# Loads of y and x1 and the stores of the output moved to one queue, normalisation one step earlier

## The reference

```
x1  = x  + layernorm(window_attention(layernorm(x) @ w_qkv))
y   = layernorm(x1), looked at as 8192 tokens
g   = mean over a batch's tokens of (relu(y @ gate_w1.T + b) @ gate_w2.T + b)      # 8 numbers a batch
mW1 = W1 + sum_e g[e] * TW1[e];   mW2 = W2 + sum_e g[e] * TW2[e]                    # per batch
out = x1 + layernorm(gelu(y @ mW1.T + mb1) @ mW2.T + mb2)
```

## Time and profile before

| | |
|---|---|
| median of 3 runs | 3098.09 us |
| profiled execution, its time | 3096.61 us |
| its span, first to last instruction | 3094.8 us |
| mean granted TensorE clock | 0.973 of full speed |
| TensorE busy, share of the span | 94% |
| VectorE, ScalarE, GpSimd busy | 64%, 49%, 28% |
| SyncE's DMA queue, ScalarE's, GpSimd's: MB moved | 631, 138, 34 |

### The profile page before, as it was taken

How to read it: one execution, slowest core, us unless ns; L and a number is a source line. 1 busy time by engine, 2 the same in 40 slices (tenths; PEclk the granted TensorE clock), 3 DMA queues, 4 the chain that set the end, 5 groups by cost and what they waited for, 6 DMA issues and landing times. The chain is left out here.

```text
span 3094.8 us, 55878 instructions
## 1 busy us (share of the span) xinstructions
PE 2912.5 (94%) x20402; PEld 2416.9 (78%) x20402; DVE 1986.4 (64%) x3730; ACT 1503.6 (49%) x2918; POOL 865.4 (28%) x725
## 2 busy tenths in 40 slices
PE   7999999789999999949986999989999999999997
PEld 5888888578888888837764888878888888888886
DVE  4333333278878888858747777788668766887412
ACT  2222222166666667645532554554445544554444
POOL 0000000178888888843310000140004100230004
PEclk9999999889999999979997999999999999999999
DMA  5554554568877777769979999999989988999533
GB/s 190 176 176 163 179 195 166 163 166 195 195 182 195 191 190 199 174 192 364 370 274 352 387 389 348 361 367 403 348 301 354 368 306 314 362 376 362 196 105 123
DMA packets 436839, 805.98 MB, mean 260 GB/s; under 512 B 28520, under 2 KB 160616, under 8 KB 436600
## 3 DMA queue, kind: packets, MB, share of 16 engines
q1 hardware_dynamic: 358208, 630.94, 61.6%
q10 hardware_dynamic: 69696, 138.42, 12.5%
q0 software_dynamic: 8704, 33.56, 3.0%
HBM read 634.51 MB, written 167.78 MB: 259 GB/s over the span
## 5 line engine op out<-in xcount | busy, mean ns | idle before, releaser
L1461 DVE SCALAR_TENSOR_TENSOR e_part<-ring,e_g_cols,e_part 128x512 f32<-128x512 f32 x896 | 649.3, 783 | 16.8 <-DMA ring<-mix_rows 13.8
L666 DVE TENSOR_REDUCE b_neg_max<-b_ps_score 128x1 f32<-128x384 f32 (+1 forms) x1024 | 491.8, 527 | 69.0 <-PE b_ps_score L531 57.4
L1372 ACT ACTIVATE e_u<-e_hid,e_mb 128x512 f32<-128x512 f32 x256 | 176.6, 690 | 636.0 <-PE e_hid L1314 631.4
L637 ACT ACTIVATE b_probs<-b_ps_keys 128x384 f32<-128x384 f32 (+1 forms) x1024 | 427.0, 479 | 80.0 <-PE b_ps_keys L546 52.0
L1312 PE MATMUL e_hid<-e_y_hi,e_w_hi 128*128 128x512 f32 x1024 | 402.5, 393 | 33.1 <-DVE e_w_lo L1472 29.9
L1482 DVE TENSOR_TENSOR e_u_lo<-e_u,e_u_hi 128x512 fp32r<-128x512 f32 x256 | 180.6, 706 | 368.2 <-ACT e_u_hi L1376 368.2
L1330 PE MATMUL e_acc<-e_w_hi,e_u_hi 128*128 128x512 f32 x1024 | 400.0, 391 | 11.8 <-ACT e_acc L1396 9.7
L1313 PE MATMUL e_hid<-e_y_lo,e_w_hi 128*128 128x512 f32 x1024 | 401.3, 392 | 0.0
L1314 PE MATMUL e_hid<-e_y_hi,e_w_lo 128*128 128x512 f32 x1024 | 401.2, 392 | 0.0
L1332 PE MATMUL e_acc<-e_w_hi,e_u_lo 128*128 128x512 f32 x1024 | 399.8, 390 | 0.0
L1331 PE MATMUL e_acc<-e_w_lo,e_u_hi 128*128 128x512 f32 x1024 | 399.6, 390 | 0.0
(11 more groups left out here) (123 smaller groups left out, 5112.9 us busy)
## 6 DMA issues: line engine op xcount, KB each, us to landing
ring<-mix_rows SPq DMA_DIRECT2D x576, 512.0 KB, 8.7
e_y_hi<-yh_scratch ACTq DMA_DIRECT2D x66, 1024.0 KB, 10.3
e_y_lo<-yl_scratch ACTq DMA_DIRECT2D x66, 1024.0 KB, 17.1
qk_scratch<-a_qk SPq DMA_DIRECT2D x128, 512.0 KB, 2.7
b_k_st<-qk_scratch SPq DMA_DIRECT2D x192, 256.0 KB, 4.3
b_q_st<-qk_scratch SPq DMA_DIRECT2D x192, 256.0 KB, 4.2
a_x_in<-x SPq DMA_DIRECT2D x16, 1024.0 KB, 7.2
v_scratch<-a_v SPq DMA_DIRECT2D x64, 256.0 KB, 3.0
```

The lines of the kernel that those rows point to most:

```text
L637: act.activation(probs[:, m % RING, h, 0:(hi - lo) * WIN], ps_keys[x % BANKS][:, 0:(hi - lo) * WIN], ACT.Exp, scale=SCALE).then_inc(exp_do ...
L666: dve.tensor_reduce(neg_max[:, g % 2, i, h:h + 1], ps_score[y % BANKS][:, 0:(hi - lo) * WIN], AX_X, ALU.max, negate=True).then_inc(reduced, 1)
L1461: dve.scalar_tensor_tensor(out=part[:, n % 2, half, :], in0=ring[:, i % RING, half * D:(half + 1) * D], scalar=g_cols[:, b, e:e + 1], in1= ...
```

## The change

- All loads of y are issued by SyncE. `load_y(r + 2)` stands behind the refills of step `last[r] - 1`, with a wait for `hidden(last[r])`. ScalarE issues no DMA any more.
- The loads of x1 and the stores of the output are issued by SyncE too: x1 behind the refills of step `last[r]`, with a wait until the adds of the closing run before are done; the stores as four of 256 KB, behind step `last[r] + 5`, each with a wait for its tile's add. Of the last two runs, the stores stand at the end of SyncE's program.
- `normalise` stands at step `last[r] + 2` instead of `+ 3`.

```diff
-        def load_y(eng, r):
-            for src, dst in ((yh_dram, y_hi), (yl_dram, y_lo)):
-                eng.dma_start(dst[:, r % 2].bitcast(F32),
-                              src[:, tokens(r)].rearrange("(k p) t -> p k t", p=P)).then_inc(y_loaded[r % 2], 16)
...
+                def load_y(r):
+                    if r >= 2:
+                        sp.wait_ge(hid_done, last[r - 2] + 1)
+                    for src, dst in ((yh_dram, y_hi), (yl_dram, y_lo)):
+                        sp.dma_start(dst[:, r % 2].bitcast(F32),
+                                     src[:, tokens(r)].rearrange("(k p) t -> p k t", p=P)).then_inc(y_loaded[r % 2], 16)
...
+                def load_x1(r):
+                    if closed_before(r):
+                        sp.wait_ge(added, TILES * closed_before(r))
+                    else:
+                        sp.wait_ge(mb2_stored, 16)
+                    sp.dma_start(x1[:, :, :], x1_dram[tokens(r), :].rearrange("(t p) d -> p t d", p=P)).then_inc(x1_loaded, 16)
+                def store_out(r):
+                    for t in range(TILES):
+                        at = chunk_of(r) * CH + t * P
+                        sp.wait_ge(added, TILES * closed_before(r) + t + 1)
+                        sp.dma_start(out[at:at + P, :], sums[:, runs[r][1], t, :]).then_inc(out_stored, 16)
...
                 for s, (r, jj) in enumerate(steps):
                     refill(upto[s - 1] if s else EXPERTS * START, upto[s])
                     for run in range(RUNS):
+                        if s == last[run] - 1 and run + 2 < RUNS:
+                            load_y(run + 2)
+                        if s == last[run] and closes(run):
+                            load_x1(run)
+                        if s == last[run] + 5 and closes(run):
+                            store_out(run)
...
-                sp.wait_ge(out_stored, 16 * PER * BATCH)
+                for run in range(RUNS):
+                    if last[run] + 5 >= STEPS and closes(run):
+                        store_out(run)
+                sp.wait_ge(out_stored, 16 * TILES * PER * BATCH)
...
-                def load_x1(r):
-                    pool.dma_start(x1[:, :, :], x1_dram[tokens(r), :].rearrange("(t p) d -> p t d", p=P)).then_inc(x1_loaded, 16)
...
-                        pool.wait_ge(added, TILES * (at + 1))
-                        pool.dma_start(out[tokens(r), :].rearrange("(t p) d -> p t d", p=P), sums[:, runs[r][1]]).then_inc(out_stored, 16)
-                        if at + 1 < len(closing):
-                            load_x1(closing[at + 1])
...
-                    r = steps[s][0]
-                    if s == last[r] and r + 2 < RUNS:
-                        load_y(act, r + 2)
...
-                        if s == last[r] + 3 and closes(r):
+                        if s == last[r] + 2 and closes(r):
                             normalise(r)
```

More of the change, by code:

```diff
@@ L1224, in _ @@
                     sp.dma_start(dst, src).then_inc(bias_loaded, 16)
-                load_y(sp, 0)
+                load_y(0)
                 sp.wait_ge(bias_done, BATCH + 1)
@@ L1230, in _ @@
                 refill(0, EXPERTS)
-                load_y(sp, 1)
+                load_y(1)
                 refill(EXPERTS, EXPERTS * START)
@@ L1247, in _ @@
                 pool.wait_ge(const_done, 3)
-                def load_x1(r):
-                    pool.dma_start(x1[:, :, :], x1_dram[tokens(r), :].rearrange("(t p) d -> p t d", p=P)).then_inc(x1_loaded, 16)
-                closing = [r for r in range(RUNS) if closes(r)]
-                pool.wait_ge(mb2_stored, 16)
-                load_x1(closing[0])
                 for r in range(RUNS):
@@ L1383, in copy_out @@
                     if opens(r) and batch_of(r) and t == 0:
-                        act.wait_ge(out_stored, 16 * (PER * (batch_of(r) - 1) + runs[r][1] + 1))
+                        act.wait_ge(out_stored, 16 * TILES * (PER * (batch_of(r) - 1) + runs[r][1] + 1))
                     act.activation(sums[:, runs[r][1], t, :], acc[t][:, :], ACT.Copy).then_inc(copied, 1)
```

## The result

The changed kernel takes 3232.64 us (median of 4 runs, 3218.83 to 3240.12) against 3097.35 us of the kernel before on the same chip. The ratio is 1.0433, with a 95% interval of 1.0394 to 1.0471. The forecast was 3133 us with a range to 3178: the sign was right and the size off by almost four times (35 us expected, 135 measured).

The account below looks back on a forecast made before the run. TensorE was taken as the bound, with the DMA engines right behind in the first batch. Losses 38 + 8 + 10 less gains 21 gave 35 us on 3096.6, so 3131.6, as median 3133; range 3100 to 3178.

Parts of the forecast that it names:

- U: In the last phase, the start of the activation behind the first `hidden` of run r + 1; issue times count from it.
- the 9.7 us wait: TensorE's single wait on an accumulator's start values in the last phase; expected to go, with 2.3 us of half clock.
- The end of the kernel: Last run's adds and store: x1 arriving sooner and a smaller last store would end the span 6.1 us earlier.
- The gains together: Last phase: start-values wait 9.7, its clock 2.3, old waits on y 3.1 and the end 6.1, together 21 us.
- The clock: TensorE's granted clock falling behind ten of the 15 short-run stalls, 1.0 us each: 10 us lost, bounds 0 and 17.
- Short runs: 15 loads of y for 3-step runs: 1.5 us stall each, plus third mix pairs and `low_weights`; 38 us lost.
- Long runs: 51 loads of y for 4-step runs: mostly in time, 8 us lost over 24 with three mix pairs, bounds 0 to 36.
- rival 1: Last phase: stalls on y stay at the lower bound, queue empty, clock holds; no change, 3097 us; chance 0.14.
- rival 2: Last phase: y is on time and the gains stay, so faster, 3077 us; chance 0.07.
- Rival 3: Last phase: y stands behind a queue of ring loads on SyncE's queue, much slower, 3184 us; chance 0.14.
- Rival 4: Last phase: the queue makes no difference, y still lands in 17 to 19 us; over 3350 us; chance 0.03.
- Rival 5: End of the first batch: moving x1 fixes nothing, 12 us more, 3145 us; chance counted within the forecast's 0.62.

Follow-up runs that it names:

- experiment 7: The changed kernel with y issued after the step's last mix but ahead of its two to four ring loads: 3132.49 us, ratio 1.0137.
- experiment 9: The changed kernel with y on SyncE's queue ahead of the refills of step `last[r] - 2`, issued when its buffer comes free: 3075.47 us, ratio 0.9945.
- experiment 10: The same as experiment 9, but with `normalise` back at step `last[r] + 3`: 3073.79 us, ratio 0.9944.
- experiment 5: The kernel before with only `normalise` moved, to step `last[r] + 2`: 3086.51 us, ratio 0.9981.
- experiment 1: The changed kernel with the loads of y back on ScalarE's queue at step `last[r]`, the rest as changed: 3080.84 us, ratio 0.9946.
- experiment 3: The changed kernel with y one step earlier on SyncE's queue, behind the refills of step `last[r] - 2`: 3092.11 us, ratio 0.9986.
- experiment 8: The changed kernel with 180 extra matmuls, 12 ahead of each wait for y in the 15 short-run cases, results thrown away: 3203.19 us, ratio 1.0352.
- experiment 2: The kernel before with only the loads of y moved to SyncE's queue, behind the refills of step `last[r] - 1`: 3238.50 us, ratio 1.0458.

## Why the prediction was wrong in its size

**Right.** When y is needed (U + 13.4), and in 13 of the 15 short-run cases when it is issued (U + 5.1 to 7.6, where the sum had U + 5.4 to 7.9). That all 15 short-run cases stall. That the 9.7 us wait goes. That a load waits for what is ahead on its queue: experiment 7. The end of the kernel came 6.1 us sooner, as forecast, but two errors cancel in it: the last adds start 2.5 us behind `normalise` instead of 1.5, and the span ends 2.5 us behind the adds instead of 3.5. The gains together were put at 21 us; experiments 9 and 10, without the loss, gain 16 to 18 in the median and 21 to 22 in the span of one execution (3073.9 and 3072.5 from 3094.8). Their parts are less sure: the wait and its clock were put at 12 us and gave 5.9 when removed alone (experiment 5).

**The step that failed** is the sum of the losses: 38 + 8 + 10 = 56 us were expected, and the runs showed about 158. The mechanism, a load of y issued too late for TensorE, was right, and experiments 1, 3 and 9 show it; three terms were too small.

*The clock: 10 expected, about 52 measured* (1464.2 us busy within the phase in the changed kernel against 1412.0 in experiment 9, where nothing stalls on y; 2.0 us for each of 26 waits, 2.3 for each of the 23 behind which the clock fell). I had a row that gave 1.7 us for one gap and wrote 1.0 for ten stalls, because a gap of 1.8 us had cost nothing. With the short stalls 2.0 us longer than I thought (67.9 / 15 = 4.5 against 38 / 15 = 2.5) and eleven long ones, the ten became 23. It was the largest error of all, and experiment 8 shows half of it (26.6 us) by itself. My upper bound of 17 us was too low for the same reason. The Trainium skill, page "TensorE: Matmul & The Clock Gate", section "HAM oscillation — how this bites in real kernels", tells of the same loss: a stream of matmuls that waits for data in each round falls back to the slow clock and pays for the transition every time. The rows agree in the main, with 0.50 in the window behind the wait of 5.85 us, but the clock did not fall behind every wait: 3.23 us here and 3.27 in experiment 7 left it at 1.00.

*Short runs: 38 expected, 67.9 measured* (2.28 to 11.47 us, 15 waits). The main part is the 1.2 us for what is ahead in the queue. In the mean of the 15 loads the pair lands 11.1 us after its issue, where I had 8.3 + 1.2 = 9.5: about 25 us of the error. Experiment 7, with the step's ring loads behind y, comes to 9.5 us, so these loads cost 1.6; the other 1.2 over the undisturbed pair are older ring loads in flight and whatever else the full DMA engines had, which I have not separated. The rest is the issue in two cases, r = 17 and 18 (U + 8.7 and 13.0): I had let GpSimd's adds slow VectorE in the long runs only, and put SyncE's waits on the adds at nothing. The longest wait, 11.47 us, is r = 18; its y_lo landed in 10.8 us like the others, only issued late.

*Long runs: 8 expected, 37.9 measured* (11 waits of 0.3 to 5.6 us). I had seen the mechanism, VectorE late while GpSimd adds, and the stores in the queue, but spread it over 24 loads at a third of a us each. It takes few loads and takes them hard: seven of the eleven were issued at U + 9.3 to 13.6, where the sum had at most U + 7.9, and two landed in 15 to 16 us. Together with the clock a stall of 5 us costs about 7.

**The rivals.** 1 and 2 are out (the 1.4 us that rival 2 names as the point of decision is 1.5 by the forecast's own terms; nothing hangs on it). Rival 3 came nearest (3184). Its term for the short runs, 70 us with 3.3 us ahead of y, is what was measured (67.9, with 2.8), and SyncE did come late behind the adds where the first batch closes. But there was no standing queue of ring loads (their median landing fell from 8.7 to 7.0 us), SyncE's waits on the adds are not needed for a loss of this size (experiment 2), and its clock term of 17 us was far too small as well. Rival 4, that the queue makes no difference, is wrong for the landing (10.7 instead of 17.1) and right in a way that I had not weighed: with lead enough, either queue gives the same time. That is also what the Trainium skill says on the page "DMA: Bandwidth & Descriptors", section "Issuing engines are not separate DMA queues": a second issuer saves only the time of issuing. Experiments 1 and 9 (0.9946 and 0.9945) agree. Rival 5 is out: the wait at the end of the first batch went.

**Left open.** How the 1.2 us of landing that remain in experiment 7 divide, and why the clock fell behind one wait and not behind another of the same length. In experiment 3 seven waits for y are left, and they (10.1 us) and 7.4 us more busy time within the phase account for its 17 us to experiment 9. Two stand at short runs (r = 6 and 7, issued at U + 2.9 and 3.5), three at loads issued near U + 8 where a batch closes, and two at loads issued in time that took 17 us to land; what held these five I did not follow.

## What to carry to other kernels

A load's place in an in-order queue is a time: it is issued when the slowest thing ahead of it on that queue has been waited for. When a DMA is moved to another engine's queue, write down what that queue waits for just before it, and compare the issue time with the last moment at which the data can still arrive, not the landing time alone. Price the clock by the number of TensorE's stalls as well as by their length: here 26 stalls, all but two of 2.2 to 11.5 us, cost about 2 us more each, and in experiment 7, where most were under 2 us, 0.7. If a kernel stalls in every round, first count the rounds. An edit that moves many things at once can hold a gain and a loss: here 0.5% of gain (experiment 1) lay under 5% of loss.

## What the runs showed of the hardware that was not expected

- Behind waits of 2.28, 3.31 and 5.85 us TensorE's granted clock was 0.56, 0.50 and 0.50 in the next window of 3 us, and the `hidden` behind them took 1.5 to 1.8 us longer than the usual 2.7 (2.5 behind one of 3.04 us). But waits of 3.23 us in the changed kernel and of 2.73 and 3.27 us in experiment 7 were followed by 1.00, and one of 2.09 us in experiment 7 by 0.50. The length of the wait alone does not tell what follows.
- More matmuls made the kernel faster (experiment 8, 25 us by the ratios, for 180 matmuls whose result nobody reads).
- Two MB on the queue of the ring land in 11 us with the ring loads around them, on a queue of their own in 17. On the ring's queue (r = 5) the second MB lands 2.7 us behind the first, as on the empty queue (2.6); on ScalarE's queue before the change the medians of the two are 7 us apart (10.3 and 17.1, from issues 0.5 us apart). The transfer that shares its queue waits first and then runs at about the undisturbed rate.
- Six mixes of VectorE took 8.21 us beside GpSimd's adds and 4.06 without them; the four adds took 6.79 us, where they took 4.92 at the end of the kernel.
